# Graph network kernel: who copies the gather indices in the first two edge passes

## The reference, cut to what matters

```python
h = relu(layernorm(x)); x = x + gru_layer(h)        # first edge pass
    src_h = h[src] @ W_msg.T + b_msg
    messages = segment_sum(src_h + edge_embed[edge_type], dst)
    h_new = gru_cell(messages, h, ...)
h = relu(layernorm(x)); x = x + gcn_layer(h)        # second edge pass
    deg = segment_sum(ones, dst) + 1
    agg = segment_sum(norm[row] * norm[col] * x[row], col)
    out = layernorm(agg @ W.T + b) * gamma + beta
...                                                  # a relation layer, then an attention layer
```

## Time and profile before

| what | value |
|---|---|
| device time, median of 3 runs | 10886.74 us (10877.73 to 10894.94) |
| profiled execution, span on the core | 10879.4 us |
| first gathers to last, first pass (line 721) | starts 133.0 to 2490.4 us |
| first gathers to last, second pass (line 988) | starts 2537.8 to 4920.8 us |
| GpSimd busy over the span | 6900.4 us (63%) |
| TensorE busy | 7281.4 us (67%) |
| VectorE busy | 4894.6 us (45%) |
| ScalarE busy | 1925.5 us (18%) |

### The profile page before, as it was taken

One profiled execution on the slowest core, in us unless ns is written; L12 is line 12 of the kernel. 1 busy time (PEld: TensorE's weight loads), 2 busy tenths in 40 slices (PEclk: granted clock), 3 DMA queues, 4 the chain that ended last, 5 costly groups with the idle time before them and its releaser, 6 DMA issues. The chain is left out here.

```text
span 10879.4 us, 143542 instructions
## 1 busy us (share of the span) xinstructions
PE 7281.4 (67%) x34582; PEld 5619.6 (52%) x34582; DVE 4894.6 (45%) x12591; ACT 1925.5 (18%) x5149; POOL 6900.4 (63%) x6291
## 2 busy tenths in 40 slices
PE   2555555554666666668888888888836666666667
PEld 2444444443333333336777777777724555555555
DVE  5444444444665565654222222222264555555556
ACT  1111111111111111112222222222221111111111
POOL 3666666665666666665888888888815555555553
PEclk6555555555555555556777777777755555555555
DMA  6222222222222222223444444444472222222222
GB/s 236 56 56 58 57 56 58 55 57 59 74 71 74 75 71 76 71 75 66 56 56 55 56 56 56 55 56 56 53 212 67 68 68 65 67 66 67 65 66 52
DMA packets 809417, 765.69 MB, mean 70 GB/s; under 512 B 128472, under 2 KB 701362, under 8 KB 809073
## 3 DMA queue, kind: packets, MB, share of 16 engines
q0 software_dynamic: 375872, 414.65, 22.5%
q1 hardware_dynamic: 340391, 271.94, 8.2%
q10 hardware_dynamic: 92938, 77.03, 2.3%
HBM read 544.72 MB, written 224.78 MB: 71 GB/s over the span
## 5 line engine op out<-in xcount | busy, mean ns | idle before, releaser
L1412 POOL DMA_INDIRECT scat<-msg_out,msg_idx x1564 | 2414.3, 1544 | 491.5 <-issue 319.8
L2001 POOL DMA_INDIRECT soft_rows<-proj,soft_slot x1564 | 1487.5, 951 | 1385.1 <-DVE soft_x L2188 718.2
L721 POOL DMA_INDIRECT L_rows<-H,L_slot x1568 | 1493.2, 952 | 993.3 <-issue 596.3
L988 POOL DMA_INDIRECT L_rows<-H,L_slot x1568 | 1496.5, 954 | 890.4 <-issue 464.5
L1505 PE MATMUL msg_ps_msg<-msg_hb,msg_lhs 128*128 128x128 f32 x6272 | 1600.9, 436 | 1.2 <-DVE msg_lhs L1478 1.2
L1505 PEld LDWEIGHTS msg_ps_msg<-msg_hb,msg_lhs 128*128 128x128 f32 x6272 | 1493.0, 328 | 185.3 <-issue 183.9
L1478 DVE SCALAR_TENSOR_TENSOR msg_lhs<-msg_dst_sp,msg_node,msg_ps_c 128x512 f32<-128x512 f32 x784 | 551.2, 745 | 2040.4 <-ACT msg_dst_sp L1433 1813.0
L2130 PE MATMUL soft_ps_sum<-soft_onehot,soft_x 128*128 128x64 f32 x3136 | 752.8, 422 | 306.0 <-DVE sums_b L2247 216.9
L861 PE MATMUL L_sum<-L_onehot,L_rows 128*128 128x64 f32 x3136 | 691.0, 392 | 392.9 <-issue 337.6
L2130 PEld LDWEIGHTS soft_ps_sum<-soft_onehot,soft_x 128*128 128x128 f32 x3136 | 705.6, 328 | 371.3 <-issue 276.8
L861 PEld LDWEIGHTS L_sum<-L_onehot,L_rows 128*128 128x128 f32 x3136 | 657.9, 305 | 433.9 <-issue 423.6
(11 more groups left out here) (365 smaller groups left out, 10133.3 us busy)
## 6 DMA issues: line engine op xcount, KB each, us to landing
L_rows<-H,L_slot POOLq DMA_INDIRECT x3136
msg_hb<-HB SPq DMA_DIRECT2D x392, 128.0 KB
soft_at_in<-in_edge_attr_dram SPq DMA_DIRECT2D x195, 256.0 KB
scat<-L_zeros SPq DMA_DIRECT2D x64, 408.0 KB
rel_parts<-scat SPq DMA_DIRECT2D x100, 256.0 KB, 5.2
HB<-L_prod ACTq DMA_DIRECT2D x49, 512.0 KB
scat<-msg_out,msg_idx POOLq DMA_INDIRECT x1564
soft_rows<-proj,soft_slot POOLq DMA_INDIRECT x1564
```

What stands on the lines that cost most here:

```text
L721: pool.indirect_dma_start(rows[:, k, j, :], None, t["H0"], bass.IndirectOffsetOnAxis(ap=slot[:, k, j:j + 1], axis=0)).then_inc(gathered[k] ...
L988: pool.indirect_dma_start(rows[:, k, j, :], None, t["H1"], bass.IndirectOffsetOnAxis(ap=slot[:, k, j:j + 1], axis=0)).then_inc(gathered[k] ...
L1412: pool.indirect_dma_start(t["scat"][j], bass.IndirectOffsetOnAxis(ap=idx[:, k, j:j + 1], axis=0), out[:, k, j, :], None, compute_op=ALU.ad ...
L2001: pool.indirect_dma_start(rows[:, s % SC, j, :], None, t["proj"], bass.IndirectOffsetOnAxis(ap=slot[:, s, j:j + 1], axis=0)).then_inc(gath ...
```

## The change

The copy of the indices moves from ScalarE to GpSimd, in both passes. GpSimd waits for `multiplied` itself, copies the four columns of the group into its slot, raises `idx_ready`, waits for that same semaphore and issues the four indirect DMAs. ScalarE's `give_indices` goes, with its place eight groups ahead. The number of slots, the semaphore values and all other stages stay. In the first pass the last, empty group gets no copy, since `gather` returns ahead of it.

```diff
@@ sum_gru_phase, gpsimd: gather @@
                 k = s % R
                 if empty(i, w, s):
                     return
+                pool.wait_ge(multiplied, r * GB + s + 1)
+                pool.tensor_copy(slot[:, k, :], t["src_i"][:, ds((i * GB + s) * J, J)]).then_inc(idx_ready, 1)
                 pool.wait_ge(idx_ready, r * GB + s + 1)
                 pool.nop(nofuse=True)
                 for j in range(J):
@@ sum_gru_phase, scalar @@
-            def give_indices(i, r, w, s):
-                act.wait_ge(multiplied, r * GB + s + 1)
-                act.activation(slot[:, s % R, :], t["src_i"][:, ds((i * GB + s) * J, J)], ACT.Copy).then_inc(idx_ready, 1)
...
-            with_nodes(act, S, t, [(R, give_indices)],
+            with_nodes(act, S, t, [],
                        [(0, stage_sums), (1, copy_turned), (2, copy_message), (6, sigmoids), (8, tanhs), (11, roots), (13, normed)])
@@ sum_gcn_phase, scalar @@
-            def give_indices(i, r, w, s):
-                act.wait_ge(multiplied, r * GB + s + 1)
-                act.activation(slot[:, s % R, :], t["src_i"][:, ds((i * GB + s) * J, J)], ACT.Copy).then_inc(idx_ready, 1)
...
-            with_nodes(act, S, t, [(R, give_indices), (0, store_coefficients)],
+            with_nodes(act, S, t, [(0, store_coefficients)],
```

## The result

The changed kernel takes 10777.72 us (median of 4 runs, 10766.11 to 10785.58) against 10882.24 us for the kernel before (4 runs, 10867.06 to 10894.94): ratio 0.9906, 95% interval 0.9892 to 0.992. Forecast was 10742. That is on a chip where the kernel before takes about 10880 us. The experiments met chips where it takes 9336 and 9321 us. One of its four executions there took 11982 us, where the other three took 9939 to 9943, and it is left out of that ratio.

A forecast was written before the change was run, and what follows sets the result against it. GpSimd's gather issue, stopped for 822 us, was taken to pace both passes. 784 groups x 5.67 = 4445, + 137 for kept stops + 15 for ends = 4597 against 4742 us, 145 less: 10742 us, range 10560 to 11220.

The forecast's parts named there:

- The likeliest case: Both gather passes: signals pass at the borders and most stops go; 10742 us, own range 10520 to 10860, chance 0.50.
- GpSimd paces both passes, and ScalarE is not late: Gather passes before: GpSimd sets the time, stopped for 822 us, while ScalarE idles waiting for TensorE's signal.
- The copy, 0.13 us, and a hand-over of 0.07: Each group border: with 0.77 us to the gather, less the old 0.30, 0.67 us more per border.
- A group takes 5.67 us: Four gathers plus the longer border where GpSimd paces, 5.56 to 5.99 us, against 6.05 on average before.
- Signals pass once a group, stops go but for 98, costing 137 us: Group borders: the pause lets TensorE's signals through; one 1.4 us stop stays per loop body of eight groups.
- Nothing else inside a pass: Both passes: beyond groups and kept stops, only 15 us were added, for the starts and ends.
- The hop is worth 0.1 us a stop: Dropping ScalarE between signal and gather saves at most 0.1 us at 281 stops, 28 us.
- Why signals pass: 0.11 us of arrears per gather, worked off in the border: Runs of gathers: something served in 1.36 us per gather lags; 0.67 us more border clears a group's 0.44 us.
- VectorE's additions wait under 5 us for remote signals: VectorE's additions in the profile after: waits called remote shrink from some 8 us to under 5.
- The stops stay: Rival at the borders: signals need a longer quiet, stops remain, 309 us more, 11196 us; chance 0.28.
- A fixed rate: Rival in both passes: about 6.05 us a group regardless, no change, 10887 us; chance 0.14, shared with a copy eating the gain.
- A dearer copy: Rival at the borders: a lock or switching cost makes 1.3 us per border, no stops, 11099 us; chance 0.08.

The follow-up runs named there:

- pause_only: Kernel before, ScalarE still giving the indices, plus a GpSimd scratch copy nobody reads and a wait for it at each group border: 10795.37 us, ratio 0.9916.
- one_ahead: Changed kernel with GpSimd copying the next group's indices ahead of this group's gathers; against the kernel before: 10841.2 us, ratio 0.996; second time 0.9947.
- change_again: The changed kernel unaltered, run on a chip where the kernel before takes 9320.9 us: 9943.08 us, ratio 1.0668.
- border_133: Kernel before plus a GpSimd fill of 128x512 and a wait for it at each group border, on a chip without stops: 10202.11 us, ratio 1.093.
- half_rows: Kernel before with each gather of both passes fetching 256 of 512 bytes per row, on a chip without stops: 9335.64 us, ratio 0.9998.
- border_070: Kernel before plus a GpSimd fill of 128x512 at each border, its wait always passed, on chips without stops: 9652.81 us, ratio 1.0339; again 1.0336.
- spread_140_again: Kernel before plus a GpSimd fill of 128x200 ahead of every gather, second run, on a chip with stops: 10966.33 us, ratio 0.9972.

## Why the prediction was right

The likeliest case came true on the chip that it was made for, 36 us above the forecast and inside its own range. The mechanism held in its outcome (a pause at each border, most stops gone), while the reason given for it did not, and the sign holds only on such chips, which the prediction could not know: that much was luck. Step by step:

- *GpSimd paces both passes, and ScalarE is not late.* ScalarE is not: `pause_only` gains nearly as much with ScalarE's part left whole, and `one_ahead`, which has no ScalarE in it, keeps 240 stops. GpSimd does pace the changed kernel, where it waits for 95 of 4623 us. In the kernel before it is stopped for 823 us, and on such chips TensorE's signals are late and TensorE itself too; the prediction looked at the signals alone, and how much each makes of the 823 us is not known.
- *The copy, 0.13 us, and a hand-over of 0.07.* The sum is right, the parts are not: the copy takes 0.20 us and starts at once. The 0.77 us before the gather were right. Border 0.97 us, 0.67 more than before, as forecast.
- *A group takes 5.67 us.* 5.70: the first gather after a pause takes 0.97, not 0.95 us, 24 us in all, which was not forecast.
- *Signals pass once a group, stops go but for 98, costing 137 us.* 68 stops are left, of 95 us: 42 less. The stops that stay are of one length, 2.3 to 2.6 us from gather to gather for 59 of 67 over 1.3 us, whether after 16 gathers or after 96.
- *Nothing else inside a pass.* Wrong by 46 us: 34 gaps of 1.66 us inside groups. The kernel before already had 7 and 8 such gaps of 1.3 to 1.7 us, which the prediction passed over; `pause_only`, `change_again` and `border_133` have 17 a pass, `half_rows` and `border_070` none: all 17 come only with GpSimd's wait for an operation of its own. What they are is open.
- Sum: 784 x 5.70 = 4469, + 95 + 46 = 4610, and 13 for the ends and small delays, 4623 against the forecast's 4597. The first pass's last gather starts at 2446.0, not at 2418.
- *The hop is worth 0.1 us a stop.* 0.1 to 0.2 by `one_ahead`, once the shorter way from its copy to the gather is taken off. With 68 stops left it hardly enters.
- *Why signals pass: 0.11 us of arrears per gather, worked off in the border.* The outcome fits, the figure doesn't: with 1.39 us from gather to gather there should have been no stops, and `spread_140_again` has 177. The gathers' packets do not fall behind, and TensorE idles between its own instructions. That part of the reasoning is refuted in its size and unproven in its kind.
- *VectorE's additions wait under 5 us for remote signals.* 4.9 us (212 times) after 7.8 (156 times) before:

```profile
DVE sums_a L801 <- remote: 1047.2, 212, 12.8
```

The rivals. *The stops stay*: 213 of 281 went, where 130 had to go to break even. Its place and price were right, though, and on the other chips it is the sign that came true, for a reason that it didn't have: there were no stops to remove, and all 784 borders grew. *A fixed rate* is refuted as it was put, no change and 10850 to 10920 us. A looser form stands: on the chips with stops all kernels take 5.90 to 6.12 us a group, and on the others 5.01 to 6.15, as GpSimd's own work sets it. A border that takes GpSimd itself over 6 us a group would test it on a chip with stops; `border_133` was made for that and ran on the other kind. *A dearer copy* is refuted; its sum of 784 x 6.3 takes the 1.3 us as an addition to the border, not as the border. The Trainium skill (SBUF — State Buffer, "SBUF: two separate sides") has an exclusive lock between VectorE and GpSimd; the prediction estimated 0.15 us a copy from it. The copies' shortest is 185 ns, their median 196 and 194: if there is such a wait, it is some 0.01 us for most copies here. One copy is the exception, the first of the second pass:

```profile
2491.03 13.70 POOL L984 COPY L_slot<-src_i 128x4 int32 x1 [1.03 <-issue]
...
2492.93 10.94 DVE L1065 MEMSET sums_c<- 128x13056 f32 x1 [2.67 <-issue]
...
2503.78 0.91 DVE L1067 CAST L_src_f<-src_i 128x1568 f32<-128x1568 int32 x1
```

It ends at 2504.73, 0.04 us after VectorE's cast that follows its long fill. The kernel before has a first gather of 12.57 us beside the same fill. So GpSimd is held up by more than ten us beside that fill, once and in both kernels. The copy starts 1.9 us ahead of the fill and no run took the fill away, so the cause is not shown.

What stays open: what on some chips makes TensorE's instructions and signals late while gathers go out every 1.25 us, and what a border must have to help. A border of 0.70 us alone would tell a pause from a mean spacing, but it was run only on chips without stops.

## What to carry to other kernels

Before you tune a wait, ask whether the waiting time is the program's or the chip's: run the same kernel on several chips. Here 823 us of the kernel were waits that are absent on other chips of the same type, and the change that trims them costs 6.7% where they are missing. On an engine that issues gathers back to back, a small operation is nearly free as long as nothing waits for it, and it costs 0.7 us as soon as the next gather waits for it; run it a group ahead. When a change moves work and adds a pause, try the pause alone: it may be the whole effect.

## What the runs showed of the hardware

- The same kernel takes 10884 and 10996 us on two chips and 9336 and 9321 us on two others. The slower chips differ by stops in the gather passes. In the kernel before, 238 of the 260 stops for which a change of `multiplied` is recorded are ended by one that comes after the last packet of the gathers, by 1.2 and 1.0 us in the median of the two passes.
- On the slower chips TensorE idles between matmuls that no wait separates (71 times over 0.3 us in the first pass before, 111 times after the change), and 390 of 642 recorded changes of its semaphore (kernel before) come over 0.9 us after the matmul. On the faster ones neither occurs: no such idle time in the 1176 places of the first pass, every change within 0.5 us.
- On such a chip a pause of 0.97 to 1.00 us after four gathers takes away about three quarters of the stops; 0.36 us do not, and 1.39 us from gather to gather take away a third and shorten the rest.
- After a wait on an operation of its own, GpSimd's next gather starts 0.77 to 0.80 us later, whether the operation took 0.20 or 0.54 us; after a satisfied wait it is 0.16 us.
- A 1x1 fill of 0.09 us between two gathers leaves their spacing at 1.25 us, a fill of 0.28 us makes it 1.39.
